# One transposition for the low-rank factors of two blocks

## The reference

```python
x = x + einsum('bct,bcd->bdt', x, w0[adapter])           # mixes the 64 tokens of a batch
x = x + x @ W1 + (x @ A1[adapter]) @ B1[adapter]         # rank 16
x = x + x @ W2.T + 0.5 * (x @ A2[labeler]) @ B2.T        # rank 32
logits = x @ Wr.T + 5 * onehot(language)         # 8 experts
gates = softmax over the top 2 of logits
x = x + x @ W3.T + 2 * sum_e gates_e * (x @ A3_e) @ B3_e # rank 16 each
```

## Time and profile before

| | |
|---|---|
| median of 3 runs | 521.8 us (520.9 to 521.87) |
| the profiled execution | 521.43 us, its span 519.6 us |
| PE busy | 515.1 us (99%) |
| DVE, ACT, POOL busy | 334.2, 201.9, 170.2 us |
| inner pairs (2 to 6) | 34.13 to 34.14 us each |
| clock granted to PE | full in all 40 slices |

### The profile page before, as it was taken

The page is one execution under the profiler, slowest core; times in us unless marked ns, Lnnn a source line. Parts: engine busy times, 40 slices in busy tenths (PEclk is TensorE's granted clock), DMA queues, the critical chain, the costliest instruction groups (busy, mean ns, idle before and its releaser), DMA issues.

```text
span 519.6 us, 8870 instructions
## 1 busy us (share of the span) xinstructions
PE 515.1 (99%) x2720; PEld 450.4 (87%) x2720; DVE 334.2 (64%) x655; ACT 201.9 (39%) x351; POOL 170.2 (33%) x250
## 2 busy tenths in 40 slices
PE   8999999999999999999999999999999999999997
PEld 8999999988988888888887888888888888888886
DVE  4798886799533333399876864756647557476464
ACT  5744653345222222267344233323333333233322
POOL 2550000002102020219546544354254434552400
PEclk9999999999999999999999999999999999999999
DMA  7911210214430202040703303313233042222312
GB/s 263 374 65 40 60 40 1 82 40 125 158 112 0 82 0 82 0 166 4 242 2 118 121 23 119 100 47 108 83 117 121 34 117 86 69 87 81 120 32 81
DMA packets 29631, 46.80 MB, mean 90 GB/s; under 512 B 12052, under 2 KB 17940, under 8 KB 29476
## 3 DMA queue, kind: packets, MB, share of 16 engines
q1 hardware_dynamic: 29268, 45.72, 27.3%
q0 software_dynamic: 192, 0.59, 0.3%
q10 hardware_dynamic: 144, 0.13, 0.1%
HBM read 33.39 MB, written 13.04 MB: 89 GB/s over the span
## 4 chain that ended last, share of the span: by engine, by line
PE 98%; DVE 1%; ACT 0%; issue 0%; POOL 0%; POOLq 0%; DVEq 0%; ACTq 0%
PE bank L1893 26%; PE bank L1827 15%; PE bank L1759 11%; PE bank L1882 8%; PE bank L1801 6%; PE bank L1730 5%; PE bank L1813 5%; PE bank L1973 4%; PE bank L1941 4%; PE bank L1949 4%; PE bank L1714 3%; PE bank L1944 1%; PE bank L1943 1%; PE bank L1903 1%; PE bank L1721 1%; PE bank L1930 0%
## 5 line engine op out<-in xcount | busy, mean ns | idle before, releaser
L1893 PE MATMUL bank<-t_hi,em_hi 128*128 128x512 f32 x168 | 57.3, 403 | 0.0
L1183 DVE TENSOR_TENSOR w1t_lo<-raw,w1t_hi 128x1024 fp32r<-128x1024 f32 x18 | 24.1, 1339 | 23.6 <-ACT w1t_hi L909 17.1
L684 POOL TENSOR_TENSOR tmp<-raw 128x512 f32<-128x512 f32 x4 | 7.2, 1793 | 97.2 <-DVE raw L1369 97.2
L1893 PEld LDWEIGHTS bank<-t_hi,em_hi 128*128 128x128 f32 x168 | 31.1, 188 | 7.2 <-DVE em_hi L1183 0.4
L1827 PE MATMUL bank<-te,em_hi 128*128 128x512 f32 x144 | 34.9, 395 | 0.0
L1827 PEld LDWEIGHTS bank<-te,em_hi 128*128 128x128 f32 x144 | 27.0, 188 | 6.6
L670 POOL CAST em_hi<-tba 128x256 fp32r x32 | 13.4, 447 | 58.3 <-PE bank L1882 54.6
L1183 DVE TENSOR_TENSOR em_hi<-tmp,em_hi 128x512 fp32r<-128x512 f32 x22 | 15.1, 688 | 21.7 <-ACT em_hi L1016 12.6
L674 POOL TENSOR_TENSOR em_lo<-tba,em_hi 128x256 fp32r<-128x256 f32 x32 | 27.1, 868 | 2.4 <-POOL em_hi L670 1.2
L1759 PE MATMUL bank<-em_hi,w2s_hi 128*128 128x384 f32 x80 | 27.0, 337 | 0.0
L1759 PE MATMUL bank<-em_lo,w2s_hi 128*128 128x384 f32 x80 | 26.9, 337 | 0.0
(11 more groups left out here) (309 smaller groups left out, 1615.2 us busy)
## 6 DMA issues: line engine op xcount, KB each, us to landing
raw<-in_x_dram SPq DMA_DIRECT2D x16, 512.0 KB, 4.2
b1s<-b1scr SPq DMA_DIRECT2D x32, 217.5 KB, 2.8
raw<-in_b1w_dram SPq DMA_DIRECT2D x10, 512.0 KB, 3.6
out_dram<-ef SPq DMA_DIRECT2D x16, 256.0 KB, 2.1
out_dram<-ost SPq DMA_DIRECT2D x15, 256.0 KB, 2.5
graw<-in_w3a3wr_dram SPq DMA_DIRECT2D x4, 768.0 KB, 11.0
b1scr<-b1stage SPq DMA_DIRECT2D x12, 256.0 KB
w2raw<-in_w_dram SPq DMA_DIRECT2D x6, 384.0 KB, 6.8
```

Of the source, the lines that this page charges most:

```text
L1183: V.tensor_tensor(dst, src, f32(hi), ALU.subtract).then_inc(signal, 1)
L1893: ins = nc.tensor.matmul(to[:, :], left[a][:, k0 + k, :], m_right(right, z, k), start=(name in OPENS and n == 0), stop=(n == 3 * KH - 1), ...
```

## The change

In pairs 2 to 6 (`JOINT`) the factors of both blocks are packed side by side. `h1c` grows to 128 columns, two blocks of 64 (high and low), and one transposition replaces two. `h2c` holds 64 columns of each block (high and low once each, before three times high and once low), and again one transposition replaces two. What was repeated in the packed tile is now repeated by ACT: 4 copies for h1 and 6 for h2 in a pair, before 2 and 2. So that the rows of `h1T` fall into this order, the two batches of a block alternate in it, and the `b1s` rows are loaded with a stride of two partitions. The orders of PE, ACT and DVE in these pairs are new: both blocks' transpositions and small products stand together in `p7` to `p4`, with one or more wide matmuls between small ones, and the routing and gates of both blocks come after them; `gated_across(b0)` moves from `p7` to the front of tile 0, and `gated_across(b1)` from there to between tiles 1 and 2. SP reads the indices for the next `b1s` loads of both blocks ahead of the output transfers. The language bias moves to another place, by two copies on POOL. The diff, cut to its core (pairs 0, 1 and 7 keep their orders):

```diff
+    H1_THREE = h1c[:, 0:2 * SEG1].rearrange("p (t r h) -> p t r h", t=3, h=PER)
+    H1_BOTH = h1c[:, :].rearrange("p (s z r h) -> p s z r h", s=2, z=2, h=PER)
+    H2_BOTH = h2c[:, :, :].rearrange("p (s z) r -> p s z r", s=2)
...
-                    for third, half in enumerate((0, 1, 0)):
+                    for third, half in enumerate((0, 0, 1)):
...
-                    rows = slice(h * SEG1, (h + 1) * SEG1)
+                    rows = slice(h, PER * SEG1, PER)
...
+                if not last:
+                    sp.wait_ge(s_idx, 48)
+                    chosen = [rows_of(2 * p + 2 + s) for s in range(2)]
...
                     if n % 2 and not last:
-                        chosen = rows_of(2 * p + 2 + s)
                         done = held(sp, 4 * p + n + 1)
                         sp.wait_ge(s_idx, 48)
                         sp.wait_ge(s_y, done)
-                        load_b1s(chosen, s)
+                        load_b1s(chosen[s], s)
...
+            pool.wait_ge(s_cst, E + 4)
+            for s in range(2):
+                nc.gpsimd.tensor_copy(BIAS[:, s, :].rearrange("p (b e) -> p b e", e=E), bias0[:, s:NB:2, :]).then_inc(s_bias, 1)
...
+            def h1_both(p):
+                act.wait_ge(s_th, th_joint(p) + 1)
+                for s in range(2):
+                    own = slice(4 * R1 * s, 4 * R1 * (s + 1))
+                    own_hi = slice(4 * R1 * s, 4 * R1 * s + 2 * R1)
+                    nc.scalar.activation(h1T[s][0:4 * R1, :], bank[RT][own, Z1], ACT.Copy).then_inc(s_hts, 1)
+                    nc.scalar.activation(h1T[s][4 * R1:6 * R1, :], bank[RT][own_hi, Z1], ACT.Copy).then_inc(s_hts, 1)
+            def h2_both(p):
+                act.wait_ge(s_th, th_joint(p) + 2)
+                for s in range(2):
+                    own = slice(2 * R2 * s, 2 * R2 * (s + 1))
+                    own_hi = slice(2 * R2 * s, 2 * R2 * s + R2)
+                    nc.scalar.activation(h2T[s][0:R2, :], bank[RT][own_hi, Z2], ACT.Copy).then_inc(s_hts, 1)
+                    nc.scalar.activation(h2T[s][R2:2 * R2, :], bank[RT][own_hi, Z2], ACT.Copy).then_inc(s_hts, 1)
+                    nc.scalar.activation(h2T[s][2 * R2:4 * R2, :], bank[RT][own, Z2], ACT.Copy).then_inc(s_hts, 1)
...
+                h1_both(p)
+                act.wait_ge(s_wide, made + PRODUCT["p7"])
+                left_hi(p + 1)
+                h2_both(p)
+                xm_hi(0, bank[BA])
+                exp_of(b0)
+                act.wait_ge(s_wide, made + PRODUCT["p3"])
+                xm_hi(1, bank[BD_])
+                exp_of(b1)
+                ght_hi(b0, 0)
+                xn_hi(b0 + 2, YB + 1, 6 * p + SMALL["mixed", 1])
+                act.wait_ge(s_add, 3 * p)
+                act.wait_ge(s_mix, 4 * p + 1)
+                xm_hi(0, bank[BC])
+                ost_even(p, 0)
+                act.wait_ge(s_wide, made + PRODUCT["p4"])
+                act.wait_ge(s_mix, 4 * p + 2)
+                xm_hi(1, bank[BB])
+                ght_hi(b1, 1)
+                ost_even(p, 2)
...
+            def first_joint(s, there, steps):
+                nar = bank[RT + s]
+                dve.wait_ge(s_small, there)
+                for h in range(PER):
+                    ts, at_ = slice(h * T, (h + 1) * T), C3 + PER * R2 + h * R1
+                    steps.then(V.tensor_copy(H1_BOTH[ts, s, 0, :, h], nar[ts, at_:at_ + R1]))
+                steps.hold()
+                for h in range(PER):
+                    ts, at_ = slice(h * T, (h + 1) * T), C3 + PER * R2 + h * R1
+                    lo(H1_BOTH[ts, s, 1, :, h], nar[ts, at_:at_ + R1], H1_BOTH[ts, s, 0, :, h], s_h1c)
+            def second_joint(s, there, steps):
+                nar = bank[RT + s]
+                dve.wait_ge(s_small, there)
+                for h in range(PER):
+                    ts, at_ = slice(h * T, (h + 1) * T), C3 + h * R2
+                    steps.then(V.tensor_scalar(H2_BOTH[ts, s, 0, :], nar[ts, at_:at_ + R2], SCALE2, None, ALU.mult))
+                steps.hold()
+                for h in range(PER):
+                    ts, at_ = slice(h * T, (h + 1) * T), C3 + h * R2
+                    V.scalar_tensor_tensor(H2_BOTH[ts, s, 1, :], nar[ts, at_:at_ + R2], SCALE2, f32(H2_BOTH[ts, s, 0, :]),
+                                           ALU.mult, ALU.subtract).then_inc(s_h2c, 1)
...
+                if gh_free is not None:
+                    dve.wait_ge(s_tg, gh_free)
...
+            def joint_pair_lo(p, steps):
+                b0, b1 = 2 * p, 2 * p + 1
+                ops = OPS * p - OPS
+                operand_lo(CS[1], tmp[:, :, :], CS[0], ops + 2)
+                first_joint(0, 6 * p + SMALL["mixed", 0], steps)
+                operand_lo(DS[1], tmp[:, :, :], DS[0], ops + 3)
+                operand_lo(XB[1][:, :, :], raw[1][:, :, :], XB[0][:, :, :], ops + 4)
+                sum_p1(p)
+                operand_lo(CS[1], raw[1][:, 0:KH, :], CS[0], ops + 5)
+                sum_p5(p)
+                xn_lo(b1, YB)
+                operand_lo(XB[1][:, 0:KH, :], tmp[:, :, :], XB[0][:, 0:KH, :], ops + 6)
+                first_joint(1, 6 * p + SMALL["mixed", 1], steps)
+                second_joint(0, 6 * p + SMALL["h1", 0], steps)
+                sum_p7(p)
+                second_joint(1, 6 * p + SMALL["h1", 1], steps)
+                left_lo(p + 1)
+                route(p, 0, steps, 6 * p + SMALL["h2", 0])
+                xm_lo(0, bank[BA], 4 * p + 1)
+                gates(b0, 0, steps)
+                route(p, 1, steps, 6 * p + SMALL["h2", 1])
+                xm_lo(1, bank[BD_], 4 * p + 2)
+                ght_lo(b0, 0)
+                xn_lo(b0 + 2, YB + 1)
+                gates(b1, 1, steps, b0 + 1)
+                xm_lo(0, bank[BC], 4 * p + 3)
+                xm_lo(1, bank[BB], 4 * p + 4)
+                ght_lo(b1, 1)
+                ost_odd(p, 1)
+                ost_odd(p, 3)
...
+            def h1_both_across(p):
+                pe.wait_ge(s_h1c, 4 * p + 4)
+                nc.tensor.matmul(bank[RT][:, Z1], f32(h1c[:, :]), ident[:, :], is_transpose=True, start=False, stop=True,
+                                 skip_group_check=True).then_inc(s_th, 1)
+            def h2_both_across(p):
+                pe.wait_ge(s_h2c, 4 * p + 4)
+                nc.tensor.matmul(bank[RT][:, Z2], f32(h2c[:, :, :]).rearrange("p m r -> p (m r)"), ident[:, :], is_transpose=True,
+                                 start=False, stop=True, skip_group_check=True).then_inc(s_th, 1)
...
+            def joint_pair_products(p):
+                b0, b1 = 2 * p, 2 * p + 1
+                ops, sums = OPS * p - OPS, 3 * p - 3
+                h1_there = hts_joint(p) + 2 * H1_COPIES
+                h2_there = hts_joint(p) + COPIES
+                part("p1", 0, 5)
+                mixed(b0, 0)
+                part("p1", 5, 12)
+                pe.wait_ge(s_opl, ops + 2)
+                part("p5", 0, 12)
+                pe.wait_ge(s_opl, ops + 3)
+                part("p6", 0, 12)
+                pe.wait_ge(s_opl, ops + 4)
+                narrow(b1, second_block, YB)
+                pe.wait_ge(s_cp, 2 * p - 1)
+                part("p2", 0, 7)
+                mixed(b1, 1)
+                part("p2", 7, 12)
+                pe.wait_ge(s_add, sums + 2)
+                pe.wait_ge(s_opl, ops + 5)
+                part("p7", 0, 3)
+                h1_both_across(p)
+                part("p7", 3, 9)
+                h1_into_from(h1_there, 0, p)
+                part("p7", 9, 10)
+                h1_into_from(h1_there, 1, p)
+                part("p7", 10, 12)
+                pe.wait_ge(s_opl, ops + 6)
+                part("p3", 0, 10)
+                h2_both_across(p)
+                part("p3", 10, 12)
+                pe.wait_ge(s_add, sums + 3)
+                part("p4", 0, 7)
+                h2_into_from(h2_there, 0)
+                part("p4", 7, 8)
+                h2_into_from(h2_there, 1)
+                part("p4", 8, 12)
+                pe.wait_ge(s_opl, ops + 7)
+                narrow(b0 + 2, first_block, YB + 1)
+                gated_across(b0, 0)
+                tile(p, 0, False, False)
+                tile(p, 1, False, False)
+                gated_across(b1, 1)
+                tile(p, 2, False, False)
+                tile(p, 3, False, False)
```

More of the change, by code:

```diff
@@ L215, in cond_resid_kernel @@
     iota = small("iota", [P, E])
-    bias = small("bias", [P, NB, E])
+    bias0 = at("bias0", [P, NB, E], F32, q[0])
+    h1c = small("h1c", [P, 2 * PER * 2 * R1], F32R)
+    assert 2 * PER * 2 * R1 == NB * E
     lg = small("lg", [P, E])
@@ L413, in cond_resid_kernel, with th_before, hts_before, th_joint @@
         WARM = 12
+        JOINT = range(2, NP - 1)
+        TH_LAST, HTS_LAST = -2 * len(JOINT), 6 * len(JOINT)
+        SMALL = {n: i + 1 for i, n in enumerate((("mixed", 0), ("mixed", 1), ("h1", 0), ("h1", 1), ("h2", 0), ("h2", 1)))}
+        H1_COPIES, H2_COPIES = 2, 3
+        COPIES = 2 * (H1_COPIES + H2_COPIES)
```

(32 more changed lines are left out.)

57 lines of the change are left out of this document (42 added, 15 removed).

## The result

| | before | after |
|---|---|---|
| median | 521.34 us (5 runs, 520.9 to 521.87) | 527.39 us (5 runs, 526.76 to 527.92) |
| profiled execution, its span | 521.43, 519.6 us | 527.43, 525.6 us |
| inner pairs | 34.14 us | 35.30 to 35.32 us |

The ratio is 1.0113, with a 95% interval of 1.0102 to 1.0125: the changed kernel is 6 us slower, and this is no matter of chance. The forecast of 525.2 us had the sign and the place, and was 2.2 us short (it was built on a median of 521.8; from 521.34 it would have been 2.6).

The account below looks back on a forecast made before the run. The prediction took PE to bound the kernel, busy 34.14 of 34.14 us per inner pair. Per pair -0.21 + 0.9 = +0.69, over five pairs +3.45 us on a median of 521.8, gave 525.2 us, range 520.8 to 527.8.

Parts of the forecast that it names:

- What leaves PE: In PE's queue, one h1 and one h2 transposition fewer per pair, 0.105 + 0.115 - 0.01: 0.21 us gained per pair.
- h1: ACT's four h1 copies finish just before h1_into's weight load on PE; taken at 0, bounds 0 to 0.15 us per pair.
- h2: ACT's six h2 copies finish before the into product's load on PE, with 0.3 us of cover; taken at 0.
- DVE's tail: Both blocks' routing and gates on DVE after h2_into of b0: no reserve before tile 2, ght_lo late by 0.15 us.
- tile 2's stall: PE's wait at tile 2 for its operand from DVE: 0.9 us per pair, bounds 0.45 to 1.35.
- The hold by POOL: On DVE, gates(b1) runs into POOL's subtractions, whose instructions in flight hold it: gates takes 1.0 us more.
- the count by instructions: DVE's gates(b1) matched one by one to POOL's subtractions: begins 410.46, xm_lo for tile 2 starts 412.94, done 413.63.
- The rest at nothing: SP's earlier index reads, b1s rows at a stride of two and POOL's two bias copies: no cost or gain.
- The sum: Per pair -0.21 + 0.9 = +0.69 us, over five pairs +3.45 us, 525.2 us on the median; chance 0.56.
- ACT's copies are late as well: Rival: h1's copies cost 0.15 us per pair on top of the upper stall, +6.5 us, 528.3 us; chance 0.10.

Follow-up runs that it names:

- edit 5: The kernel before, with each h1 transposition issued three times instead of once; 524.19 us against 521.26, ratio 1.0057.
- edit 7: edit 6 with both h2 into products one wide matmul of p4 later; 520.5 us against 521.58 for the kernel before, ratio 0.9978.
- edit 6: Changed kernel with POOL waiting for b1's gates, h1 into products one matmul later, tile 0's operand split ahead of h2 copies and routing; 521.22 us, ratio 1.0000.
- edit 2: The changed kernel, but POOL starts on the second block's columns only when gh of b1 is written; 522.22 us, ratio 1.0016 to the kernel before.
- edit 8: edit 7 without POOL's wait for the second block's gates; 524.19 us, ratio 1.005 to the kernel before.
- edit 1: The changed kernel with the old orders of PE, ACT and DVE in pairs 2 to 6; 521.9 us against 521.5 for the kernel before, ratio 1.0006.

## Why the prediction was right, and where it was short

**What leaves PE: right.** 0.105 and 0.115 were read from starts, edit 5 measured 0.104 and edit 7 gave 0.22 for both, where -0.21 stood in the sum. The figure of the Trainium skill ("TensorE: Matmul & The Clock Gate", Back-to-back issue gap) would have been 0.05 too small per pair.

**h1: wrong.** "It just fits. [...] I take 0." This step failed. The copies follow each other at 0.29, not 0.22, because the row I took the spacing from was of another kind: a copy to 96 partitions with a wide activation behind it, where these go to 64 and 32. It is not the width of what follows, for the wide `xm_hi` behind the last h2 copy (407.25) starts 0.30 later too, at 407.55. Four of them end 0.21 later (3 x 0.07) than I had them, of which the sum had 0.05 in hand (399.23 against 399.28); measured 0.17 on PE per pair, beyond my bound of 0.15. The start was well placed: `h1_both_across` comes 15.24 us into the pair by the prediction (398.0, the pair beginning at 382.76), 15.26 in the trace.

**h2: right in its effect, not in its cover.** Six copies at 0.29 (5 x 0.07 = 0.35 later) used up the 0.3: in the changed kernel `h2_into`'s load waited 0.17 for ACT, and its matmul still started in its turn, at 407.68. One more activation ahead of it was enough to make it late (edit 6).

**DVE's tail: right.** From `route(b0)` to the start of `gates(b1)` the steps were to take 5.11 us, and took 413.20 - 408.08 = 5.12. `gates(b1)` was to begin 1.43 after `gated_across(b0)` and began 1.45 after it. `ght_lo` was late as said, by 0.11 where I had 0.15, but this does not add to tile 2's stall.

**The hold by POOL: right mechanism, mis-sized term.** It is shown by edit 2, where the stall goes with POOL's overlap, and by edit 8, where it comes back. "`gates` takes 1.0 us more" was 1.35, as I let one subtraction hold both `gm` and let `gate` end with the third; in fact the multiply, each of the two instructions of `gm`, and `gate` met one of POOL's each, the fourth too. This made `xm_lo` come 416.73 - 413.20 = 3.53 after the start of `gates(b1)`, where the count by instructions gave 3.17. The stall of tile 2, 0.9 in the sum, measured 1.175, inside the bounds of 0.45 to 1.35; it grew by less than the 0.36 between these two, since PE got 0.13 back when it restarted (last section). The step "a DVE instruction on SBUF operands alone waits there" was drawn too wide: the reciprocal above was not held. The Trainium skill ("GPSIMD Engine Reference", Key points) names which instructions are open to it, those in a 2-port mode or with two SBUF inputs. The trace agrees for the multiply and `gate`, with two such inputs (0.69 and 0.38, held), and for `gh`, which reads PSUM (0.29, not held). `gm`, with one tensor and two scalars per partition, was held too (0.67 and 0.51), and the reciprocal with its one input was not (0.16); which mode these run in no run here shows.

**The rest at nothing: right** (edit 1: 1.0006 [0.9997, 1.0015]). `b1s` for b1 goes out at 388.29, 2.9 us into the pair instead of 7.4, and helps nobody.

**The sum.** Per pair -0.21 + 0.9 = +0.69 was forecast; measured -0.21 + 0.17 + 1.175 + 0.04 = 1.18. Over five pairs the stall of tile 2 makes 1.4 of the missing 2.4 us, ACT's copies 0.85, what I could not place 0.2; the last is within the reading of starts. The rival "ACT's copies are late as well" had this shape, both stalls near their upper bounds, and 528.3 us; what came, 527.4, lies between it and the forecast and nearer to the rival, which had a chance of 0.10. It lies 0.4 us inside the upper end of the range: the bounds held it, not the middle.

**Open.** Why small copies on ACT stand 0.29 apart here was not tried, nor what decides which DVE instructions POOL holds. Nor was a wait of `h1_into(b0)` for its own two copies alone: PE would then write a PSUM bank from which ACT still reads. The 0.04 to 0.05 us per pair that stay in the changed kernel and in edit 2 are not there in edit 7; which of the later products removed them I don't know.

## What to carry to other kernels

When work is merged to save an instruction on the full engine, write out for each other engine when its longer burst ends against when it is needed: here 0.21 us was saved on PE, and two bursts (four copies on ACT, the routing and gates of both blocks on DVE) lost their cover. Tiny SBUF instructions on the path, of the kinds that were held here, should not be placed beside POOL's long ones; one wait that lets POOL go after them was worth 1.06 us per pair. And a spacing is to be read between instructions of the very kind that will follow each other, down to the number of partitions.

## What the runs showed of the hardware

- While an instruction of POOL is in flight, some DVE instructions, however small, last until it is over and end 0.01 to 0.03 us after it; the next one then falls under POOL's next. Held were the multiply on `gw` and `gate` (two SBUF inputs), `gm` (a tensor_scalar of 128x8) and `topf` (a cast of 128x2). Four of 0.16, 0.29 (twice, with some overlap) and 0.17 took 1.35 us more. Not held were the reciprocal (128x1, 0.16 at 294.28), the index search (0.16 at 337.80), `den` (128x1, 0.14 at 413.20, beside a cast of POOL's that ended at 413.37) and, in the pairs, those that read PSUM.
- ACT's copies of 128 columns out of PSUM to 32 or 64 partitions, one behind the other, start 0.29 to 0.30 us apart at 0.27 us each: no overlap. In the same trace a copy to 128 partitions, also out of PSUM, has the next activation 0.17 behind it:

```profile
412.06 0.28 ACT L1095 ACTIVATE ght_hi<-bank 128x128 fp32r<-128x128 f32 x1
412.23 0.36 ACT L1066 ACTIVATE em_hi<-bank 128x232 fp32r<-128x232 f32 x1
```

- A transposition of 96 columns costs PE's stream 0.104 us (edit 5), though each is recorded with 0.27 and lies under its neighbours.
- After a wait for an operand that is loaded as weights PE gets a little back: at 416.78 load and matmul start together, where in steady running the load stands 0.23 ahead, and the third matmul starts 417.34 - 416.78 = 0.56 after the load instead of 0.23 + 0.465, so 0.13 sooner. In the five pairs of the changed kernel this step is 0.56 to 0.58.
